# Cross-attention block with FFN: the residual of the quantised linears added to x by seven accumulating transfers instead of fourteen GpSimd additions

## The chip, the cores and the metric

The kernel runs on one core of one Trainium2 chip. The metric is device time in microseconds (us), taken as the median of several runs. The five engines of the core are TensorE (PE, with its weight loads shown apart as PEld), VectorE (DVE), ScalarE (ACT), GpSimd (POOL) and SyncE (SP). Each runs its own instruction stream in order, and they meet only through semaphores. Transfers run beside them on 16 DMA engines that all queues share.

## The reference, cut to what matters

```python
def smooth_quant_linear(x, w):            # x [T, D], w [O, D]
    s  = sqrt(max|x| over tokens / max|w| over rows)      # per column of D
    xs, ws = x / s, w * s
    x_q, w_q = round(xs / x_scale), round(ws / w_scale)   # scales per row, 127 levels
    return x_q @ w_q.T * x_scale * w_scale.T

def xattn(x, gate_up, ctx):               # 4 batches of 512 tokens, D = 512, I = 256
    gate, up = split(smooth_quant_linear(x, gate_up))
    return smooth_quant_linear(silu(gate) * up, ctx)

def ffn(x, ...):                          # all 2048 tokens
    pick 2 of 8 experts by the router logits summed over all tokens
    h = gelu(x @ w1[e] + b1[e]);  y = h @ w2[e] + b2[e]   # DFF = 2048
    return sum over the two experts of weight * y

x = x + xattn(layernorm(x), ...)          # the "+" is the residual of this change
x = x + ffn(layernorm(x), ...)
```

All data is float32.

## The kernel before, in words

Tokens lie on the 128 partitions, four tokens a partition and batch, so that `res` [128, 16, 512] holds x of all four batches. The program has two stages. The first, up to about 150 us, computes the two quantised linears of the four batches b = 0 to 3. The second, the FFN, works through 16 pairs of 128-wide hidden blocks; its products are split in high and low parts and multiplied with Strassen's seven products instead of eight.

The first stage is written out by hand: each engine has a list of steps such as `smooth_weight(2, 2)` (batch 2, linear 2) or `dequant(3, 2, 1)` (batch 3, linear 2, half 1), and runs them in that order. PSUM is used as four slots of two banks. Each slot has a fixed list of uses, and `drained` counts how many of them have been emptied; the helper `place` finds which slot and count a use such as `p2.1.0` (product of linear 2, batch 1, half 0) has.

The end of the first stage, for each batch: GpSimd rounds the second weight (`round_weight`, L372), TensorE transposes and multiplies (L616, L635), ScalarE copies the transposed integers out of PSUM (`integers_w`, L946), VectorE multiplies the product by its scales into `wv` (`dequant`, L1283). Then `add_residual(b, h)` (L385 to L391) on GpSimd adds half h (two of the four rows of 512 that a partition holds) of `wv` to `res`. Seven of the eight halves are done so; the last, (3, 1), is VectorE's `add_last_residual` (L1330).

The second layer norm follows. Its sums come from ScalarE for batch 0 (`moments(0, 2)`, L911 and L916) and from VectorE for batches 1 to 3 (L1217 to L1223). GpSimd's `inv_std` (L340, L341) turns them into the reciprocal of the standard deviation. The rows are normalised by ScalarE (L895), by GpSimd for batch 2 (L396) and by VectorE for half of batch 3 (L1323). TensorE transposes them (`normed2`, L656), the router's product (L667) and the choice of two experts follow, and with it SyncE's first loads of expert weights (L285, L289).

The order of GpSimd around the change is: `add_residual(0,0)`, then `smooth_weight(2,2)`, four small steps, `round_weight(1,2)`, `row_scale(2,2,1)`, `add_residual(0,1)`, `round_weight(2,2)`, `smooth_weight(3,2)`, `row_scale(3,2,0)`, `add_residual(1,0)`, `inv_std(0,2)`, `row_scale(3,2,1)`, `add_residual(1,1)`, `round_weight(3,2)`, `add_residual(2,0)`, `inv_std(1,2)`, `add_residual(2,1)`, `add_residual(3,0)`, `inv_std(2,2)`, `normalise(2)`, `inv_std(3,2)`. Those that read `res` next wait for `res_added[b]`, which each addition raises by one.

Of the kernel before, what the change touches and what calls it, by code (L numbers as in the profile page):

```python
# [5 lines left out]
ALU = mybir.AluOpType  # L6
# [17 lines left out]
def xattn_ffn(  # L24
# [16 lines left out]
    TT = T // P  # L41
# [3 lines left out]
    H = KD // 2  # L45
# [16 lines left out]
    with ExitStack() as ctx:  # L62
        def sb(name, shape, dt=F32, stack=ctx):
            return stack.enter_context(nc.sbuf_tensor(name, shape, dt))

        def sem(name):
            return ctx.enter_context(nc.semaphore(name))

        def each(name):
            return [sem(f"{name}{b}") for b in range(B)]  # L70
# [21 lines left out]
        def place(use):  # L92
            for i, uses in enumerate(SLOTS):
                if use in uses:
                    return i, uses.index(use)


        res = sb("res", [P, NT, D])
# [41 lines left out]
        def batch_sb(name, shape, dt=F32):  # L140
            return [sb(f"{name}{b}", shape, dt, early) for b in range(B)]
# [6 lines left out]
        wv = batch_sb("wv", [P, OT, D])  # L148
# [74 lines left out]
        xscale_ready, wscale_ready = each("xscale_ready"), each("wscale_ready")  # L223
        xr_ready, wr_ready = each("xr_ready"), each("wr_ready")
        silu_ready, a_ready, res_added = each("silu_ready"), each("a_ready"), each("res_added")
        hi_ready, lo_ready = each("hi_ready"), each("lo_ready")
        res_last, xn_last = sem("res_last"), sem("xn_last")
        part_ready, tok_ready, t4_sum = each("part_ready"), sem("tok_ready"), sem("t4_sum")
# [89 lines left out]
        def _(pool):  # L318
            g = nc.gpsimd
# [66 lines left out]
            def add_residual(b, h):  # L386
                slot_i, n = place(f"p2.{b}.{h}")
                pool.wait_ge(drained[slot_i], n + 1)
                for j in range(H * h, H * h + H):
                    r = res[:, b * TT + j, :]  # L390
                    g.tensor_tensor(r, r, wv[b][:, j, :], ALU.add).then_inc(res_added[b], 1)  # L391

            def normalise(b):
                pool.wait_ge(nmr_ready[b], 2)
# [50 lines left out]
            gate_up_product(3, 1)  # L445
            root(2, 2)
            add_residual(0, 0)
            smooth_weight(2, 2)
            row_scale(2, 2, 0)
# [3 lines left out]
            round_weight(1, 2)  # L453
            row_scale(2, 2, 1)
            add_residual(0, 1)
            round_weight(2, 2)
            smooth_weight(3, 2)
            row_scale(3, 2, 0)
            add_residual(1, 0)
            inv_std(0, 2)  # L460
            row_scale(3, 2, 1)
# [427 lines left out]
        def _(act):  # L889
# [10 lines left out]
            def summed(ins):  # L900
                sums[0] += 1
                ins.then_inc(mom_link, 1)
                act.wait_ge(mom_link, sums[0])

            def moments(b, c):
                if c == 1:
                    act.wait_ge(x_load[b], 16)
                for j in range(TT):
                    if c == 2:
                        act.wait_ge(res_added[b], j + 1)  # L910
                    ins = s.activation(xv[b][:, j, :], res[:, b * TT + j, :], ACT.Identity,  # L911
                                       accum_out=mv[b][:, j, 0:1])
                summed(ins)
                summed(s.mul(nmean[c - 1][b][:, :], mv[b][:, :, 0], -1.0 / D))
                for j in range(TT):
                    ins = s.activation(xv[b][:, j, :], res[:, b * TT + j, :], ACT.Square,  # L916
                                       bias=nmean[c - 1][b][:, j:j + 1], accum_out=mv[b][:, j, 1:2])
                summed(ins)
                s.activation(var_e[c - 1][b][:, :], mv[b][:, :, 1], ACT.Copy, bias=LN_EPS, scale=1.0 / D
                             ).then_inc(var_ready[b], 1)  # L920
# [89 lines left out]
            normalise(0, 1)  # L1010
            normalise(1, 1)
            moments(2, 1)
            keep_smooth_row(0, 1)
            moments(3, 1)
            normalise(2, 1)
            keep_smooth_row(1, 1)
# [48 lines left out]
            integers_w(1, 2, 0)  # L1065
            keep_scale_row(2, 2)
            moments(0, 2)
            integers_w(2, 2, 0)
            round_x(3, 2)
# [113 lines left out]
        def _(dve):  # L1183
# [4 lines left out]
            def link(ins):  # L1188
                chain[0] += 1
                ins.then_inc(dve_link, 1)  # L1190
                dve.wait_ge(dve_link, chain[0])
# [17 lines left out]
            def moments(b, c):  # L1209
                if c == 1:  # L1210
                    dve.wait_ge(x_load[b], 16)
                for j in range(TT):
                    if c == 2 and b == B - 1 and j >= H:
                        dve.wait_ge(res_last, j - H + 1)
                    elif c == 2:
                        dve.wait_ge(res_added[b], j + 1)
                    ins = v.bn_stats(stats[b][:, j, :], res[:, b * TT + j, :])  # L1217
                link(ins)
                for j in range(TT):
                    ins = v.bn_aggr(mv[b][:, j, :], stats[b][:, j, :])  # L1220
                link(ins)
                v.tensor_scalar(nmean[c - 1][b][:, :], mv[b][:, :, 0], -1.0, None, ALU.mult)
                v.tensor_scalar(var_e[c - 1][b][:, :], mv[b][:, :, 1], LN_EPS, None, ALU.add).then_inc(var_ready[b], 1)  # L1223
# [168 lines left out]
            dve.sem_inc(comb_ready, 15)  # L1392
            dve.sem_inc(h_ready, 4)
            moments(0, 1)
            amax_w(0, 0)
            moments(1, 1)
            amax_w(0, 1)
            amax_x(0, 0)
# [89 lines left out]
            dequant(2, 2, 0)  # L1488
            dequant(2, 2, 1)
            moments(1, 2)  # L1490
            dequant(3, 2, 0)
            dequant(3, 2, 1)
# [133 lines left out]
```

## Time and profile before

| what | value |
|---|---|
| median of three runs | 820.07 us (819.11 to 821.62) |
| profiled execution, its span | 818.7 us |
| what the median has above that span | 1.4 us |
| TensorE busy | 771.5 us, 94% |
| VectorE busy | 477.7 us, 58% |
| GpSimd busy | 449.7 us, 55% |
| ScalarE busy | 354.6 us, 43% |
| mean granted TensorE clock | 0.979 of full speed |

The span runs from the first to the last instruction of one profiled execution. For that execution no time is listed beside its span, so the span is its own time here. Busy shares are averages over both stages: in the page's 40 slices of 20.5 us, TensorE is at 50 to 80% in the first seven and at 90% or more from there on. A step of the first stage costs time only if it is on the chain that leads to the FFN's start.

### The profile page before, as it was taken

What the parts mean: (1) busy time and instruction counts of PE and PEld (TensorE: products, weight loads), DVE (VectorE), ACT (ScalarE), POOL (GpSimd) and SP (SyncE); (2) the same over time, 40 slices, a digit from 0 to 9 for tenths busy, and PEclk for the clock granted to TensorE, in tenths of its full rate; (3) what the DMA queues carried; (4) which work ended last, traced back from release to release, by engine and by line L of the source; (5) the groups of instructions that cost most, each with busy time, mean ns of one, the idle gap of its engine ahead of it and who ended that gap; (6) DMA issues with size and microseconds to landing.
All of it is one profiled execution on the core that took longest, in us unless ns stands there. A gap on an engine that the chain in (4) does not pass through costs nothing.

```text
span 818.7 us, 11342 instructions
## 1 busy us (share of the span) xinstructions
PE 771.5 (94%) x3570; PEld 624.1 (76%) x3577; DVE 477.7 (58%) x669; ACT 354.6 (43%) x660; POOL 449.7 (55%) x497
## 2 busy tenths in 40 slices
PE   5688666999999999999999999999999999999998
PEld 4666455688788888888888888888888888888886
DVE  5999759797754545454545454545454545454545
ACT  3967588743442434343424343434343434242422
POOL 1789997157564646464646464646464646464622
PEclk9899968999999999999999999999999999999999
DMA  9400000301010101010101010101010101010022
GB/s 344 173 2 1 1 0 2 129 1 51 1 52 1 51 0 49 3 50 2 48 4 51 1 45 6 42 9 44 7 41 11 36 15 36 15 32 19 0 103 104
DMA packets 19077, 32.34 MB, mean 39 GB/s; under 512 B 872, under 2 KB 11240, under 8 KB 18160
## 3 DMA queue, kind: packets, MB, share of 16 engines
q1 hardware_dynamic: 18896, 31.98, 11.1%
q8 instruction: 12, 0.20, 0.1%
q10 hardware_dynamic: 160, 0.08, 0.0%
q14 instruction: 9, 0.07, 0.0%
HBM read 27.87 MB, written 4.19 MB: 39 GB/s over the span
## 4 chain that ended last, share of the span: by engine, by line
PE 83%; POOL 8%; DVE 3%; issue 2%; ACT 2%; DMA 1%; ACTq 0%; POOLq 0%; DVEq 0%
PE slot L805 42%; PE slot L792 34%; PE slot L850 3%; POOL wv L366 2%; POOL xf L383 1%; PE slot L667 1%; POOL wv L372 1%; POOL cv L366 1%; PE slot L585 1%; DVE rmax L1226 1%; DMA b_rows<-in_L_ffn_b 1%; POOL rstd L340 1%; POOL h_lo L476 1%; DVE stats L1217 1%; DVE peak_x L1226 1%
## 5 line engine op out<-in xcount | busy, mean ns | idle before, releaser
L792 PE MATMUL slot<-xo,a_hi 128*128 128x512 f32 x840 | 259.1, 390 | 0.0
L1541 DVE SCALAR_TENSOR_TENSOR res<-slot,rw,res 128x512 f32<-128x512 f32 x256 | 178.5, 750 | 130.3 <-PE slot L805 130.2
L1570 DVE TENSOR_TENSOR e<-slot,e 128x512 f32<-128x512 f32 x150 | 103.8, 692 | 173.4 <-PE slot L792 173.3
L805 PE MATMUL slot<-w_hi,h_hi 128*128 128x512 f32 x512 | 201.3, 393 | 0.4 <-POOL h_lo L476 0.4
L805 PE MATMUL slot<-w_lo,h_hi 128*128 128x512 f32 x512 | 199.6, 390 | 0.0
L805 PE MATMUL slot<-w_hi,h_lo 128*128 128x512 f32 x512 | 199.4, 390 | 0.0
L792 PEld LDWEIGHTS slot<-xo,a_hi 128*128 128x128 f32 x840 | 157.4, 188 | 33.3 <-DVE e L1570 0.2
L476 POOL TENSOR_TENSOR h_lo<-e,h_hi 128x512 fp32r<-128x512 f32 x96 | 138.1, 1451 | 55.0 <-ACT e L1104 54.0
L792 PE MATMUL slot<-xo,a_lo 128*128 128x512 f32 x420 | 163.7, 390 | 0.0
L805 PEld LDWEIGHTS slot<-w_hi,h_hi 128*128 128x128 f32 x512 | 96.1, 188 | 25.1 <-POOL h_lo L476 5.6
L476 POOL TENSOR_TENSOR h_lo<-hid,h_hi 128x512 fp32r<-128x512 f32 x32 | 44.1, 1378 | 124.7 <-ACT hid L1104 124.7
L805 PEld LDWEIGHTS slot<-w_hi,h_lo 128*128 128x128 f32 x512 | 96.2, 188 | 20.1
L805 PEld LDWEIGHTS slot<-w_lo,h_hi 128*128 128x128 f32 x512 | 96.2, 188 | 19.3
L792 PEld LDWEIGHTS slot<-xo,a_lo 128*128 128x128 f32 x420 | 78.9, 188 | 16.5
L1103 ACT ACTIVATE h_hi<-e,b_now 128x512 fp32r<-128x512 f32 x90 | 64.9, 721 | 58.0 <-DVE e L1570 57.6
L1142 ACT COPY e<-slot 128x512 f32<-128x512 f32 x30 | 17.6, 587 | 164.5 <-PE slot L792 164.5
L490 POOL TENSOR_TENSOR a_lo<-raw,a_hi 128x256 fp32r<-128x256 f32 x45 | 34.3, 761 | 95.9 <-ACT a_hi L988 95.9
L991 ACT CAST w_hi<-raw 128x512 fp32r<-128x512 f32 x32 | 19.8, 622 | 109.8 <-PE slot L805 109.8
L495 POOL TENSOR_TENSOR w_lo<-raw,w_hi 128x512 fp32r<-128x512 f32 x30 | 38.7, 1289 | 50.4 <-ACT w_hi L991 50.4
L1104 ACT ACTIVATE e<-e,b_now 128x512 f32<-128x512 f32 x90 | 63.8, 709 | 0.0
L1103 ACT ACTIVATE h_hi<-slot,b_now 128x512 fp32r<-128x512 f32 x38 | 26.2, 689 | 66.5 <-PE slot L792 56.6
L490 POOL TENSOR_TENSOR a_lo<-ssum,a_hi 128x256 fp32r<-128x256 f32 x60 | 43.7, 739 | 0.0
(145 smaller groups left out, 814.5 us busy)
## 6 DMA issues: line engine op xcount, KB each, us to landing
raw<-in_L_ffn_w SPq DMA_DIRECT2D x32, 512.0 KB, 3.4
res<-in_x SPq DMA_DIRECT2D x4, 1024.0 KB, 11.9
wv<-in_fside_BxS2xS SPq DMA_DIRECT2D x4, 1024.0 KB, 12.8
out_x<-res SPq DMA_DIRECT2D x3, 1024.0 KB, 3.9
cv<-in_ctx SPq DMA_DIRECT2D x4, 512.0 KB, 13.1
out_x<-res SPq DMA_DIRECT2D x4, 256.0 KB, 2.7
b_row<-in_L_ffn_b SPq DMA_DIRECT2D x2, 256.0 KB, 4.6
b_rows<-in_L_ffn_b ACTq DMA_DIRECT2D x1, 64.0 KB, 6.0
```

Source lines behind the costliest of these rows:

```text
L366: g.tensor_tensor(w[:, j, :], w[:, j, :], rows[b][:, 0:n], ALU.mult).then_inc(wmul_ready[b], 1)
L476: g.tensor_tensor(h_lo[:, i, :], hid[i][:, :], h_hi[:, i, :].bitcast(F32), ALU.subtract).then_inc(h_ready, 1)
L490: g.tensor_tensor(a_lo[:, i, :, :], A_OF[i], a_hi[:, i, :, :].bitcast(F32), ALU.subtract).then_inc(a_ops_ready, 1)
L495: g.tensor_tensor(w2_lo[:, f, :], raw2[:, f, :], w2_hi[:, f, :].bitcast(F32), ALU.subtract).then_inc(w2_ready, 1)
L792: last = t.matmul(dst, a[:, i, k, :], xo[tp][:, v, k, :], start=(start and n == 0), stop=(n == 3 * H - 1), skip_group_check=True)
L805: last = t.matmul(y_bank[j][:, :], a[:, i, j * P:(j + 1) * P], v[:, f, :], start=(start and n == 0), stop=(not start and n == 2), skip_gro ...
L850: last = t.matmul(TILE_BANK[n], a[:, 2 * f + h, k, :], xo[q][:, v, k, :], start=(m == 0), stop=(m == 3 * KD - 1))
L991: s.copy(w2_hi[:, f, :], raw2[:, f, :]).then_inc(w2_hi_ready, 1)
L1103: s.activation(h_hi[:, i, :], src, ACT.Gelu_apprx_tanh, bias=bias).then_inc(hid_ready, 1)
L1104: s.activation(hid[i][:, :], src, ACT.Gelu_apprx_tanh, bias=bias).then_inc(hid_ready, 1)
L1541: v.scalar_tensor_tensor(out=r, in0=y_bank[j][:, :], scalar=rw[:, ds(p, 1), n:n + 1].rearrange("p a b -> p (a b)"), in1=r, op0=ALU.mult, o ...
L1570: v.tensor_tensor(dst[:, :], src, other[:, :], ALU.add).then_inc(comb_ready, 1)
```

## The change

A half's two additions by GpSimd, each of 128 x 512 elements, become one transfer, issued by GpSimd, that reads 128 x 1024 elements (512 KB) of `wv` and adds them to `res` at the destination. Its completion raises a semaphore by 16. There are now two semaphores for each batch, one for each half, and the readers wait for 16 on the one of their half. The order of steps on every engine stays as it was; VectorE's own addition of the last half stays too.

```diff
+        res_added2 = each("res_added2")
...
             def add_residual(b, h):
                 slot_i, n = place(f"p2.{b}.{h}")
                 pool.wait_ge(drained[slot_i], n + 1)
-                for j in range(H * h, H * h + H):
-                    r = res[:, b * TT + j, :]
-                    g.tensor_tensor(r, r, wv[b][:, j, :], ALU.add).then_inc(res_added[b], 1)
+                at = H * h
+                r = res[:, b * TT + at:b * TT + at + H, :]
+                g.dma_start(r, wv[b][:, at:at + H, :], accum_op=ALU.add).then_inc((res_added, res_added2)[h][b], 16)
...
                     if c == 2:
-                        act.wait_ge(res_added[b], j + 1)
+                        act.wait_ge((res_added, res_added2)[j // H][b], 16)
...
                     elif c == 2:
-                        dve.wait_ge(res_added[b], j + 1)
+                        dve.wait_ge((res_added, res_added2)[j // H][b], 16)
```

The instructions of GpSimd's queue from the rounding of batch 3's second weight to the second layer norm's last `inv_std`, before; the names ending in a digit are those of a batch:

```order
L391 TENSOR_TENSOR res<-res,wv 128x512 [waits drained2]
L391 TENSOR_TENSOR res<-res,wv 128x512
L372 TENSOR_SCALAR cv<-cv,rscale 128x256 [waits wscale_ready3]
L372 TENSOR_SCALAR cv<-cv,rscale 128x256 x3
L391 TENSOR_TENSOR res<-res,wv 128x512 [waits drained3]
L391 TENSOR_TENSOR res<-res,wv 128x512
L340 TENSOR_TENSOR rstd_1<-var_e_1,neg_half 128x4 [waits var_ready1]
L341 TENSOR_TENSOR nmr_1<-nmean_1,rstd_1 128x4 [waits pool_link]
L391 TENSOR_TENSOR res<-res,wv 128x512 [waits drained2]
L391 TENSOR_TENSOR res<-res,wv 128x512
L391 TENSOR_TENSOR res<-res,wv 128x512 [waits drained2]
L391 TENSOR_TENSOR res<-res,wv 128x512
```

The same place of GpSimd's queue now:

```order
L392 DMA res<-wv 128x1024 [waits drained2]
L373 TENSOR_SCALAR cv<-cv,rscale 128x256 [waits wscale_ready3]
L373 TENSOR_SCALAR cv<-cv,rscale 128x256 x3
L392 DMA res<-wv 128x1024 [waits drained3]
L341 TENSOR_TENSOR rstd_1<-var_e_1,neg_half 128x4 [waits var_ready1]
L342 TENSOR_TENSOR nmr_1<-nmean_1,rstd_1 128x4 [waits pool_link]
L392 DMA res<-wv 128x1024 [waits drained2] x2
```

Eight additions have become four DMA issues, those of (1,1), (2,0), (2,1) and (3,0). The issue for (2,1) still stands behind the `inv_std` of batch 1, which waits for that batch's variance.

## Rows read from the trace of the kernel before

**Rows 1.** The page's first and fourth parts: busy time, and the chain by engine.
```profile
PE 771.5 (94%) x3570; PEld 624.1 (76%) x3577; DVE 477.7 (58%) x669; ACT 354.6 (43%) x660; POOL 449.7 (55%) x497
...
PE 83%; POOL 8%; DVE 3%; issue 2%; ACT 2%; DMA 1%; ACTq 0%; POOLq 0%; DVEq 0%
```

**Rows 2.** Chain that ended last, in order: start us, us, what.
```profile
96.89 2.50 POOL res L391 x2
...
110.04 2.46 ACT xf L911 x8
...
133.58 3.05 POOL xf L396 x4
```

**Rows 3.** Groups by line and shape, 90 to 140 us: busy us, mean ns | idle before.
```profile
L391 POOL TENSOR_TENSOR res<-res,wv 128x512 f32<-128x512 f32 x14 | 17.5, 1271 | 0.3
```

**Rows 4.** Instructions in order of time, GpSimd: start us, us, what [idle before].
```profile
102.22 0.24 POOL L377 TENSOR_SCALAR scale<-rmax 128x4 f32<-128x4 f32 x1
...
106.80 2.49 POOL L391 TENSOR_TENSOR res<-res,wv 128x512 f32<-128x512 f32 x2
...
116.72 1.04 POOL L340 TENSOR_TENSOR rstd<-var_e,neg_half 128x4 f32<-128x4 f32 x1
...
118.43 2.50 POOL L391 TENSOR_TENSOR res<-res,wv 128x512 f32<-128x512 f32 x2
...
125.40 1.03 POOL L340 TENSOR_TENSOR rstd<-var_e,neg_half 128x4 f32<-128x4 f32 x1 [0.18 <-DVE var_e L1223]
...
126.66 4.97 POOL L391 TENSOR_TENSOR res<-res,wv 128x512 f32<-128x512 f32 x4
```

**Rows 5.** The same view, ScalarE.
```profile
111.16 0.62 ACT L911 ACTIVATE xf<-res 128x512 f32<-128x512 f32 x1
...
115.72 0.20 ACT L919 ACTIVATE var_e<-mv 128x4 f32<-128x4 f32 x1
```

**Rows 6.** The same view, VectorE.
```profile
100.63 1.22 DVE L1226 TENSOR_REDUCE rmax<-xf 128x4 f32<-128x1024 f32 x1
...
121.98 2.46 DVE L1217 BATCH_NORM_STATS2 stats<-res 128x6 f32<-128x512 f32 x4
...
125.74 2.73 DVE L1283 SCALAR_TENSOR_TENSOR wv<-slot,scale,wsc_row 128x512 f32<-128x512 f32 x4 [0.42 <-PE slot L635]
128.38 2.46 DVE L1217 BATCH_NORM_STATS2 stats<-res 128x6 f32<-128x512 f32 x4
...
132.84 2.46 DVE L1217 BATCH_NORM_STATS2 stats<-res 128x6 f32<-128x512 f32 x4
```

**Rows 7.** The same view, TensorE.
```profile
86.41 1.89 PE L635 MATMUL slot<-xf 128*128 128x512 bf16 x8
...
104.24 1.92 PE L606 MATMUL slot<-ident,xf 128*128 128x128 f32 x8
...
116.98 3.57 PE L635 MATMUL slot<-xf 128*128 128x512 bf16 x8 [4.56 <-ACT xf L946]
...
122.37 1.04 PE L616 MATMUL slot<-ident,cv 128*128 128x128 f32 x8
```

**Rows 8.** DMA view: issues by line, KB each, median us to landing.
```profile
GB/s 344 173 2 1 1 0 2 129 1 51 1 52 1 51 0 49 3 50 2 48 4 51 1 45 6 42 9 44 7 41 11 36 15 36 15 32 19 0 103 104
...
raw<-in_L_ffn_w SPq DMA_DIRECT2D x32, 512.0 KB, 3.4
...
out_x<-res SPq DMA_DIRECT2D x3, 1024.0 KB, 3.9
cv<-in_ctx SPq DMA_DIRECT2D x4, 512.0 KB, 13.1
out_x<-res SPq DMA_DIRECT2D x4, 256.0 KB, 2.7
```

**Rows 9.** Instructions in order of time, SyncE's queue.
```profile
148.99 0.39 SPq L285 DMA_DIRECT2D raw<-in_L_ffn_w  x1
```

**Rows 10.** Window 116.9 to 120.5 us: length, busy of PE, PEld, DVE, ACT, POOL, PEclk, DMA, GB/s.
```profile
116.90:120.50 3.60, 3.52 (x9) 1.40 (x10) 1.59 (x3) 3.60 (x8) 3.35 (x5) 0.50 0.00 0
```

## The prediction

> **What bounds the kernel now.** I read the page's busy times first: TensorE is busy 94% of the span and carries 83% of the chain of waits, with GpSimd second at 8% [rows 1]. The FFN is TensorE's and the change leaves it alone, so all that can move is its start, and the FFN then shifts as a block. The chain in order of time says what sets that start: between 97 and 137 us it goes from GpSimd over ScalarE back to GpSimd [rows 2]. One addition pair, that of (0,0) at 96.89 us, is a link of the chain itself. The reader should see that ScalarE's sums of batch 0 at 110.04, which read what the additions write, are a link too, and so is GpSimd's normalising at 133.58. Then I read each engine's instructions in order of time, to find how long before its reader each addition is done.
>
> **What is removed.** Fourteen additions of 1.271 us, 17.5 us of GpSimd in all [rows 3], 2.5 us a half. Seven issues take their place. How long an issue holds GpSimd no row shows. From below it is SyncE's issue, 0.39 us [rows 9]; above that lies the pair that it replaces, 2.5 us, or even the whole transfer (a rival below). I take 1.1 us more than the landing of a SyncE transfer would include, from one addition of 1.27 us as the nearest GpSimd work over 128 partitions.
>
> **Where removing it pays.** The pair at 96.89 delays `smooth_weight(2,2)` and so the row scale at 102.22. That needs VectorE's maximum, which starts at 100.63 and takes 1.22 us [rows 4, 6]; with 0.08 us of handing over it could start at 101.93. So 2.5 us less of work is worth at most 102.22 - 101.93 = 0.3 us. The pair at 106.80 lies before `round_weight(2,2)`, but the product that this feeds waits for ScalarE until 116.98 [rows 7], because the copy out of PSUM stands behind ScalarE's whole `moments(0,2)`, which ends at 115.72 + 0.20 = 115.92 [rows 5]. Nothing there. Later GpSimd gets 2 us ahead in `round_weight(3,2)`, but its transposes start at 122.37 without a wait, behind TensorE's own work [rows 7]. Nothing again. From 125.40 GpSimd waits for VectorE's variance of batch 1 [rows 4]. The gain is 0.3 us in all.
>
> **What a transfer costs.** Call L the time from the start of GpSimd's issue until the reader sees the semaphore. No row shows an accumulating transfer. The nearest is the plain load of 512 KB by SyncE, 3.4 us [rows 8]. An addition at the destination must read the destination too, 512 KB more. By the stores (1024 KB in 3.9 us, 256 KB in 2.7) that is 2 x 0.4 = 0.8 us; by the rate of the loads in the first slice, 344 GB/s, it is 1.5 us [rows 8]. I take 1.5, and 1.1 for the issue as above: L = 3.4 + 1.5 + 1.1 = 6.0 us. From below L is no less than the 2.7 us of a 256 KB store; from above 13.1 us is the context load of the same size, in a crowded queue [rows 8].
>
> The Trainium skill, "DMA: Bandwidth & Descriptors", Anatomy of one DMA (SWDGE, gpsimd path), fits a GpSimd-issued transfer as 2.0 us plus bytes over 436 GB/s. For 512 KB that estimate is 3.2 us, close to the row's 3.4 us for SyncE's; if the destination's read counts in full it is 4.4 us. No run here shows either yet. By these L would sit at the low end, and the sum below would be about 0 to +1 us.
>
> **Where the landing is awaited.** Four readers matter. Before, the addition itself took 2.5 us; now it takes L.
>
> (a) Half (0,1), read by ScalarE's third sum at 111.16 [rows 5]. It is issued at 106.80 - 0.3 = 106.5. It stalls ScalarE if 106.5 + L > 111.16, that is L > 4.66. Then `integers_w(2,2)`, the product at 116.98 and all behind it shift. The shift is s = L - 4.66, and never below -0.3. At L = 6: +1.34.
>
> (b) Half (1,1), read by VectorE's third statistic of `moments(1,2)`, 1.19 us after 121.98, so at 123.17 (+ s) [rows 6]. Its issue follows `inv_std(0,2)`, which waits for the variance at 115.92 [rows 5] where it was at 116.72 before. From there to the old pair it was 118.43 - 116.72 = 1.71 us [rows 4], so it is issued at 117.65 + s. The stall is L - 5.5. At L = 6: +0.5.
>
> (c) Half (2,1), read by VectorE's third statistic of `moments(2,2)`, at 128.38 + 1.19 = 129.57 [rows 6]. Its issue cannot move forward, because `inv_std(1,2)` is ahead of it in the queue and waits for VectorE until 125.40; so it stays at 126.66 [rows 4]. Before, the pair was done at 126.66 + 2.49 = 129.15, 0.4 us ahead of the reader. Now it lands at 126.66 + L. The stall is L - 2.9. At L = 6: +3.1. Nothing covers it. Behind the waiting statistic stand VectorE's last residual, `moments(3,2)`, the low parts, and behind those GpSimd's `inv_std`s and `normalise(2)` at 133.58, TensorE's transposes and the router: the whole way to the FFN.
>
> (d) Half (3,0), issued right behind (2,1), is read 132.84 - 129.57 = 3.3 us after it [rows 6]. One issue and the second transfer's own movement (1.5 x 2 us) fit in that. Nothing.
>
> The other halves cost nothing up to L = 7.7. (0,0) has 13 us, from 96.89 to 109.9. The pair (1,0) stood ahead of the `inv_std` at 116.72, so it began by 114.2, 7.8 us before its reader at 121.98. The pair (2,0) stood ahead of 125.40, so it began by 122.9, and now begins 2.2 us earlier (the issue at 117.65 in place of 118.43, and 1.1 us in place of 2.5): 7.7 us before 128.38 [rows 2, 4, 6].
>
> **The sum.** At L = 6: 1.34 + 0.5 + 3.1 = +4.9 us, of which the second term is partly absorbed by the 0.42 us that VectorE waited before the product at 125.74, but it comes back through `inv_std(1,2)`, so I keep it. Against the profiled execution, 818.7 + 4.9 = 823.6 us. The median of the runs stood 1.4 us above that span: 825.0 us. The slope is steep, one to three us for each us of L: L = 3.4 gives -0.3 + 0.5 = +0.2; L = 5 gives +2.4; L = 7 gives 2.3 + 1.5 + 4.1 = +7.9; L = 9 gives 4.3 + 3.5 + 6.1 = +13.9.
>
> TensorE's clock adds an uncertainty of its own. After 4.56 us of idle the product at 116.98 ran 3.57 us at clock 0.50, the lower level; eight matmuls of that kind took 1.89 us at 86.41, half as much [rows 7, 10]. A longer idle makes this no better, and may slow the transposes behind it. I leave it out of the sum and put +-1.7 us beside it.
>
> **Rivals.**
> 1. The transfer lands nearly as a plain one does, L between 3 and 5: the stalls (a) and (b) are small, (c) is 0.1 to 2.1. The rows for it are the 3.4 and 3.9 us of plain transfers [rows 8], and hardly anything else moves on the DMA engines then. Against it stands the second read and that GpSimd has to produce the issue. Time: 820.0 to 822.5 us, no change that can be told. The Trainium skill's fit above lies here.
> 2. The transfer is much slower, L of 8 or more, or GpSimd is held for the whole of it. If held at L = 6, `smooth_weight(2,2)` comes 3.5 us late, (0,1) lands at 106.8 + 3.5 + 6 = 116.3, 5.1 us after its reader; (c) costs 3.1, and (3,0) starts only when (2,1) is done, 6 - 3.3 = 2.7 more: 5.1 + 3.1 + 2.7 = +10.9, and 831 us. In this case GpSimd isn't relieved and the change doesn't do what it says. Unheld with L = 8 it is also +10.9. For it: nothing in the rows excludes it; an in-place addition is not shown at all. Against it: 512 KB is little for 16 engines.
> 3. Faster: L below about 4, and TensorE's gap of 4.56 us before 116.98 gets shorter by the 0.3 us and stays at the upper clock. Then the product costs 1.7 us less, and the transposes at 104.24, 1.92 us against 1.04 us for eight of the same size at 122.37, cost 0.9 less [rows 7]: -0.3 - 1.7 - 0.9 = -2.9, 817.2 us. It decides where L is below 4.66 (no stall of ScalarE) and the gap falls short of whatever lowers the clock; 0.3 us off 4.56 is a weak reason.
>
> **How the numbers follow.** Chances: my forecast (L of 5 to 8) 0.46, rival 1 0.32, rival 2 0.18, rival 3 0.04. The likeliest case gives 825.0 us, its own range 822.4 to 831. A measurement of this kernel can tell 0.3%, 2.5 us, from no change. Faster by more is rival 3, 0.04; within it is rival 1 with the low edge of mine, 0.32; slower is the rest, 0.64. The range takes in rival 1 from its middle and rival 2 up to 834: 820.3 to 834.
>
> **What would show it.** In the changed profile: the issue at L392 as a group of seven with its time to landing (my 6.0 less the hand-over); ScalarE's L912 waiting for a DMA at about 111 us by 1 to 2 us; VectorE's L1218 waiting for a DMA of `res` at about 130 us, some 3 us; GpSimd's busy time down by about 17 us at no gain; the FFN from TensorE's L851 on of the same length, and started 5 us later. Wrong would be: a landing under 4.5 us with no such waits, GpSimd idle or blocked for the length of a transfer at L392, or a first FFN matmul that starts earlier than before.

## The result and the profile after

The change made the kernel slower, by a third of a per cent: 823.0 us median of 17 runs against 820.07 of the kernel before, ratio 1.0032, 95% interval 1.0021 to 1.0043, that is 2.6 us; the two medians differ by 2.9. One of the 17 runs of the kernel before took 1304.35 us, and nothing here rests on it. The runs of the changed kernel also list their spans. The median span is 821.1 us, and the time lies 1.9 us above the span. The same holds for 35 runs of the kernel before that were taken beside the first experiments: 1.9 us above a median span of 818.1. The span shown in front of the prediction, 818.7, lies above its median, and that of the profile after, 819.8, below its own: this pair of profiles tells less than half of the loss in its spans, so what follows reads waits, and takes totals from the runs.

The page after, parts 1 and 6. GpSimd is busy 9.8 us less, not 17.5, because the seven issues count as its work (6.6 us) and its `normalise(2)` takes 1.0 us more, as shown below; the transfers land after 4.7 us.

```profile
PE 770.1 (94%) x3570; PEld 622.7 (76%) x3577; DVE 477.2 (58%) x669; ACT 354.4 (43%) x660; POOL 439.9 (54%) x490
...
raw<-in_L_ffn_w SPq DMA_DIRECT2D x32, 512.0 KB, 3.3
...
res<-wv POOLq DMA_DIRECT2D x7, 512.0 KB, 4.7
```

The instructions of GpSimd in the changed kernel, in order of time: start us, us, what [idle before]. They answer to [rows 4].

```profile
96.60 1.10 POOL L392 DMA_DIRECT2D res<-wv  x1
...
101.67 0.23 POOL L378 TENSOR_SCALAR scale<-rmax 128x4 f32<-128x4 f32 x1 [0.95 <-DVE rmax L1227]
...
106.22 0.95 POOL L392 DMA_DIRECT2D res<-wv  x1
...
115.74 1.04 POOL L341 TENSOR_TENSOR rstd<-var_e,neg_half 128x4 f32<-128x4 f32 x1 [2.69 <-ACT var_e L920]
...
117.44 0.97 POOL L392 DMA_DIRECT2D res<-wv  x1
...
124.95 1.04 POOL L341 TENSOR_TENSOR rstd<-var_e,neg_half 128x4 f32<-128x4 f32 x1 [3.62 <-DVE var_e L1224]
...
126.35 1.81 POOL L392 DMA_DIRECT2D res<-wv  x2
133.17 1.40 POOL L341 TENSOR_TENSOR rstd<-var_e,neg_half 128x4 f32<-128x4 f32 x1 [5.02 <-DVE var_e L1224]
...
134.96 4.07 POOL L397 TENSOR_SCALAR xf<-res,rstd,nmr 128x512 f32<-128x512 f32 x4
139.00 1.97 POOL L341 TENSOR_TENSOR rstd<-var_e,neg_half 128x4 f32<-128x4 f32 x1
```

GpSimd now waits where it worked: 0.95, 2.69, 3.62 and 5.02 us idle, each time for a value of VectorE or ScalarE. Beyond the 0.3 us of the row scale at 101.67 its freed time buys nothing. And its four rows of `normalise(2)` (L397), 3.05 us in [rows 2], take 4.07.

The same view of VectorE and ScalarE in the changed kernel, to lay beside [rows 5, 6]. This execution is 0.28 us ahead of that of before already at 93 us, where nothing has changed yet; that is to be added to its times.

```profile
127.99 1.28 DVE L1218 BATCH_NORM_STATS2 stats<-res 128x6 f32<-128x512 f32 x2
131.11 1.29 DVE L1218 BATCH_NORM_STATS2 stats<-res 128x6 f32<-128x512 f32 x2 [1.83 <-DMA res<-wv]
...
134.20 2.46 DVE L1218 BATCH_NORM_STATS2 stats<-res 128x6 f32<-128x512 f32 x4
...
137.26 2.85 DVE L1292 TENSOR_TENSOR xo<-xf,xo 128x1024 fp32r<-128x1024 f32 x2
```

```profile
110.53 0.20 ACT L912 ACTIVATION_READ_ACCUMULATOR xf<-res 128x1 f32 x1
110.88 0.63 ACT L912 ACTIVATE xf<-res 128x512 f32<-128x512 f32 x1
...
115.44 0.20 ACT L920 ACTIVATE var_e<-mv 128x4 f32<-128x4 f32 x1
```

VectorE's third statistic of batch 2 waits 1.83 us for the transfer of half (2,1): issued at 126.35, seen at 131.11, so 4.76 us. ScalarE's third sum starts 0.15 us after the read before it has ended, where it overlapped that by 0.1 us in [rows 5]: 0.25 us lost on half (0,1), issued at 106.22 and seen at 110.88 (4.66 us).

The FFN itself did not change: from its first matmul (L850 before, L851 now) to the end of the span it is 665.2 us in both, and in the profiles of the first four experiments too. The first stage makes the whole difference.

The chain of waits of the changed kernel, in order of time, names the same two transfers:

```profile
106.22 4.63 DMA res<-wv
110.88 1.35 ACT xf L912 x4
...
126.35 4.74 DMA res<-wv
131.11 1.30 DVE stats L1218 x2
...
134.96 4.07 POOL xf L397 x4
```

### The profile page after: what moved, and what is told of

Read it like the earlier page. It is cut to its first block, busy times and chain, and to the rows that moved or that the text cites. A ratio compares the mean times of both kernels' runs of the same rounds, so it can differ in the third digit from the quotient of the medians.

```text
span 819.8 us, 11335 instructions
## 1 busy us (share of the span) xinstructions
PE 770.1 (94%) x3570; PEld 622.7 (76%) x3577; DVE 477.2 (58%) x669; ACT 354.4 (43%) x660; POOL 439.9 (54%) x490
## 4 chain that ended last, share of the span: by engine, by line
PE 81%; POOL 9%; DVE 4%; issue 3%; DMA 2%; ACT 1%; ACTq 0%; POOLq 0%; DVEq 0%
PE slot L806 42%; PE slot L793 34%; PE slot L851 3%; POOL wv L367 2%; DMA res<-wv 1%; POOL xf L384 1%; POOL wv L373 1%; POOL cv L367 1%; PE slot L586 1%; DVE rmax L1227 1%; POOL rstd L341 1%; DVE stats L1218 1%; DMA b_rows<-in_L_ffn_b 1%; POOL h_lo L477 1%; DVE peak_x L1227 1%
```

## The experiments

Theory A at the start: the loss is landing time that readers wait for, nearly all of it half (2,1), whose issue stands behind an `inv_std` that waits. Theory B: a price for using the transfers at all, outside the readers' waits. Ratios are to the kernel before, run on the same chip, with 95% intervals.

**Transfer of (2,1) ahead of the inv_std of batch 1.**

```diff
             add_residual(2, 0)
-            inv_std(1, 2)
             add_residual(2, 1)
+            inv_std(1, 2)
```

> The changed kernel with one GpSimd step moved: the transfer of half (2,1) is issued ahead of the inv_std of batch 1 instead of behind it. Theory A (the loss is the landing time of (2,1), 4.76 us counted from an issue that waits behind inv_std): the issue comes at about 121.9 us instead of 126.35, lands near 126.6, VectorE's wait of 1.83 us at 131.1 is gone, GpSimd's normalise(2) no longer meets VectorE's low parts for its whole length (3.05 us again, not 4.07), and the time falls from the changed kernel's by 2 to 2.7 us, to the kernel before or 0.3 us under it (ratio 0.999 to 1.001). Theory B (the loss is a fixed price of having a seventh kind of queue, the software one, or of the transfers disturbing other engines): the wait goes but the time stays 1 us or more above the kernel before (ratio 1.0015 or more).

Measured: 0.9991 (0.9976 to 1.0005). The issue comes at 122.64. The wait for (2,1) is gone; one of 0.46 us for (3,0) is left, because that transfer took 5.7 us. One order of two steps is worth 0.4%, the whole loss: for A. How that 0.4% divides is another question. In its profile `normalise(2)` is back at 3.03 us, and TensorE's granted clock between 140 and 143 us is 1.00 where it is 0.50 in the kernel before and in the changed one. Below, VectorE and GpSimd of this run:

```profile
128.79 2.46 DVE L1218 BATCH_NORM_STATS2 stats<-res 128x6 f32<-128x512 f32 x4
...
133.60 2.47 DVE L1218 BATCH_NORM_STATS2 stats<-res 128x6 f32<-128x512 f32 x4 [0.46 <-DMA res<-wv]
...
136.85 2.35 DVE L1292 TENSOR_TENSOR xo<-xf,xo 128x1024 fp32r<-128x1024 f32 x2
```

```profile
133.82 3.03 POOL L397 TENSOR_SCALAR xf<-res,rstd,nmr 128x512 f32<-128x512 f32 x4
137.02 1.91 POOL L341 TENSOR_TENSOR rstd<-var_e,neg_half 128x4 f32<-128x4 f32 x1 [0.17 <-DVE var_e L1224]
```

**Only (2,1) added by GpSimd.** `if (b, h) not in MOVED:` the two additions as before, with MOVED all of the seven but (2,1).

> The changed kernel with only half (2,1) added by GpSimd as before, the other six by transfer. Theory A: the additions run from 126.3 to 128.8, VectorE doesn't wait, half (3,0) is issued at 128.8 and lands at 133.5, while it is read at 132.6: a wait of about 0.9 us takes the place of the 1.9, so the ratio to the kernel before is 1.0005 to 1.0015 and VectorE shows one wait for the transfer of (3,0). Theory B: ratio as of the changed kernel, 1.002 to 1.004.

Measured: 0.9990 (0.9976 to 1.0004), lower than A's range. In its profile VectorE waits 2.47 us for (3,0), more than the 0.9 expected, and yet the loss is gone. Two things can explain it, and the runs don't tell which. The wait comes one step later: GpSimd's `normalise(2)`, started by the variance of batch 2, went ahead meanwhile (133.27, 3.03 us, no collision). And the profiled execution, with a span of 819.8, was the slowest of the twelve, whose median is 817.5; its transfer took 6.1 us, which may not be so in most.

**An idle queue.** The kernel before, with one 2 KB transfer issued by GpSimd at 13 us, and a wait for it behind GpSimd's last step of the first stage (the declarations are left out here):

```diff
             inv_std(0, 1)
+            link(g.memset(spare2[:, :], 0.0))
+            g.dma_start(spare[:, :], spare2[:, :]).then_inc(spare_in, 16)
...
             inv_std(3, 2)
+            pool.wait_ge(spare_in, 16)
```

> The kernel before, all fourteen additions by GpSimd, plus one plain transfer of 2 KB that GpSimd issues at about 13 us into its idle time and that nobody reads. Theory A: no change in the span (ratio 1.0000 within 0.0005). Theory B: the use of a queue for GpSimd's transfers has a price outside the span or at its end; the time less the span grows by 0.5 us or more and the ratio is 1.0005 to 1.002.

Measured: 0.9998 (0.9985 to 1.0012), time less span 1.91 us, as without it. B is out as far as such a queue has a fixed price.

**Only (2,1) by transfer.** The reverse: MOVED is (2,1) alone, and the other six halves are added by GpSimd.

> The kernel before with only half (2,1) turned into a transfer, six halves still added by GpSimd. Theory A: this one transfer carries the whole loss. It is issued at 126.66 and lands at 131.4, against 129.57 for its reader, +1.9 us of wait; the additions of (3,0) run 127.6 to 130.1 and are in time. Ratio 1.002 to 1.004, the same as the changed kernel or 0.0003 above it (it lacks the 0.3 us gained by the other halves). Theory B: about a seventh of the loss, ratio under 1.001.

Measured: 1.0041 (1.0029 to 1.0053). One transfer of seven carries the whole loss. That the other six give anything back is not shown: this interval overlaps that of the changed kernel. Its profile has the same picture as the changed kernel: issue at 127.09, reader at 131.89, `normalise(2)` 4.08 us. So A is shown from both sides: without (2,1) no loss, with (2,1) alone all of it.

**What the landing consists of.** Three kernels, each timed once. First the addition left out (`accum_op=ALU.add` removed, so that `wv` is copied over `res`); then these copies issued by SyncE, with GpSimd doing neither additions nor issues; then the accumulating transfers cut into two of 256 KB each.

> The changed kernel with plain copies of wv over res in place of the accumulating transfers: same shapes, same GpSimd issues, but the residual's addition is left out. Theory A (the addition at the destination halves the rate at which 16 engines move the data, and that is the larger part of the landing time): DMA windows of a single transfer show about twice 197 GB/s, and the landing falls from 4.7 to 3.2 to 3.5 us. Theory B (the landing is mostly GpSimd's issue and the completion): 4.2 us or more.

> The same plain copies issued by SyncE, each behind a wait for its product's last drain; the residual's addition is left out, and GpSimd has neither additions nor issues. Theory A: SyncE's issue takes 0.4 us instead of 0.9 and the landing is 0.8 to 1.1 us shorter than in the run with GpSimd's copies, 2.3 to 2.7 us; that difference is the part of the landing that belongs to GpSimd making the transfer. Theory B: no difference, under 0.3 us.

> The changed kernel with each transfer cut in two, 256 KB each, fourteen in all, both of a half raising one semaphore to 32. Theory A (landing is a fixed part of about 2.0 us plus 512 KB at 197 GB/s, 2.7 us): a first piece lands after 3.3 us, a second one, behind it, after about 4 us; GpSimd's issue takes 0.9 us again for each piece, so the whole half lands 0.3 us later than the 4.7 us of one transfer. Theory B (landing independent of size): each piece 4.5 us or more.

Measured: 3.0 us to landing for GpSimd's copies, 2.9 for SyncE's, 4.7 for the accumulating ones; pieces of 256 KB land after 3.3 us at the least and 4.2 at the median, and the half (2,1) as a whole after 5.35 us (issued at 127.58, seen at 132.93). The DMA columns of the windows view (last three: clock, share of 16 engines, GB/s) show where the difference is. First the changed kernel, its first transfer, issued at 96.60; then the run with copies, issued at 96.71:

```profile
97.60:98.60 1.00, 0.72 (x7) 0.48 (x5) 1.00 (x2) 0.44 (x2) 0.75 (x2) 1.00 0.39 74
98.60:99.60 1.00, 0.00 (x0) 0.00 (x0) 1.00 (x2) 0.84 (x1) 1.00 (x3) 1.00 1.12 217
99.60:100.60 1.00, 0.00 (x0) 0.00 (x0) 0.97 (x2) 0.00 (x0) 1.00 (x2) 1.00 1.05 197
100.60:101.60 1.00, 0.00 (x0) 0.00 (x0) 0.98 (x1) 0.00 (x0) 0.12 (x1) 0.60 0.21 37
```

```profile
98.00:98.50 0.50, 0.43 (x4) 0.19 (x2) 0.50 (x2) 0.00 (x0) 0.44 (x1) 1.00 0.90 360
98.50:99.00 0.50, 0.00 (x0) 0.00 (x0) 0.50 (x1) 0.47 (x1) 0.50 (x2) 1.00 1.02 410
99.00:99.50 0.50, 0.00 (x0) 0.00 (x0) 0.50 (x2) 0.50 (x1) 0.50 (x2) 1.00 0.70 279
```

After the start of the issue nothing moves for 1.3 us in the copy and 1.6 us in the addition. Then all 16 engines are busy: at 410 GB/s for a copy, at 197 GB/s with the addition. 512 KB take 1.3 us at the one rate and 2.7 at the other, which is 1.4 of the 1.7 us between the landings; the later start is the other 0.3. The theory on the rate is shown; that on GpSimd's issue isn't: 3.0 against 2.9 us is 0.1, not 0.8 to 1.1. An issue holds GpSimd 0.95 us (0.6 for a copy, and SyncE 0.46), but little of that shows in the landing. The pieces took 1.13 us of issue each, and ahead of the last of them GpSimd stood for 2.9 us, which the chain of that run puts down to "issue":

```profile
130.32 2.92 issue
133.23 3.28 DMA res<-wv
136.53 2.48 DVE stats L1219 x4
```

In this run cutting the transfers up was no way out: VectorE waited 2.00 us for (2,1). The single times were 820.9 us for the copies, 816.3 for SyncE's and 823.1 for the pieces; nothing rests on them.

**Halves chosen by slack.** Transfers for (0,0), (1,0), (1,1), (2,0) and (2,1), the last ahead of `inv_std(1,2)`; (0,1) and (3,0) added by GpSimd.

> The halves chosen by their slack: (0,0), (1,0), (1,1), (2,0) and (2,1) by transfer, (2,1) issued ahead of the inv_std of batch 1, and (0,1) and (3,0) added by GpSimd, which is idle there. No engine waits for a transfer. Theory A: the 0.15 us of ScalarE and the 0.46 us of VectorE that the run with (2,1) ahead still waited are gone as well; ratio to the kernel before 0.997 to 0.9995, and 0.3 to 0.8 us under the run with (2,1) ahead. Theory B (GpSimd's own later work, normalise(2) and inv_std(3,2), ends last anyway): 0.9985 to 1.0005, no better than the run with (2,1) ahead.

Measured: 0.9993 (0.9976 to 1.0010). VectorE and ScalarE wait for no transfer, and it is no better than the run with (2,1) ahead: theory B of that expectation. `normalise(2)` took 4.09 us in its profile, which leads to the next question.

**The two low parts later.** `keep_lo` is VectorE's subtraction that leaves the low part of a split tile (L1292 in the changed kernel). In all profiles so far the first of them starts 2.3 to 2.4 us after `normalise(2)` where VectorE doesn't wait for half (3,0). Where it was 2.29 to 2.32 us (the changed kernel, the idle queue, only (2,1), the copies, the mixed one) GpSimd took 4.07 to 4.09; where it was 2.40 or more (the kernel before, SyncE's copies, and the three runs in which `moments(3,2)` came later) it took 3.01 to 3.05. The fourth row starts 2.29 us after the first. In the changed kernel that row alone lasts 1.83 us, against 0.76 of the other three. The two sides are 0.1 us apart, and the idle queue, which has none of the transfers, is on the side of the changed kernel. First VectorE's row of the kernel before, 2.40 us after its `normalise(2)` at 133.58; then GpSimd and VectorE of the idle queue, 2.32 us apart:

```profile
135.98 2.86 DVE L1291 TENSOR_TENSOR xo<-xf,xo 128x1024 fp32r<-128x1024 f32 x2
```

```profile
134.50 4.09 POOL L397 TENSOR_SCALAR xf<-res,rstd,nmr 128x512 f32<-128x512 f32 x4
...
136.82 2.85 DVE L1295 TENSOR_TENSOR xo<-xf,xo 128x1024 fp32r<-128x1024 f32 x2
```

So the seven transfers are not needed for the two to collide. Three more runs move VectorE's work away from GpSimd's: the changed kernel, the changed kernel with (2,1) ahead, and the kernel before, each with this edit.

```diff
-            keep_lo(0, 0)
-            keep_lo(1, 0)
             normalise_last()
+            keep_lo(1, 0)
             token_sums(2)
             keep_lo(1, 1)
             token_sums(3)
             token_total()
+            keep_lo(0, 0)
             keep_lo(0, 1)
```

> The changed kernel with VectorE's two first low parts, keep_lo(0,0) and keep_lo(1,0), moved behind its normalise_last. Question: does the 1.0 us by which GpSimd's fourth row of normalise(2) is longer (1.83 instead of 0.76 us) come from VectorE's subtraction beside it, and does it count? Theory A (it does): GpSimd's normalise(2) takes 3.0 us in place of 4.07, the reciprocal root of batch 3 behind it 1.0 us in place of 1.97, VectorE's wait of 1.8 us for the transfer stays, and the time falls by 1 to 2 us: ratio to the kernel before 1.0005 to 1.0025. Theory B (the lengthening is of GpSimd's own making, or what GpSimd gains is lost because the low parts come later to the router): normalise stays at 4 us, or ratio 1.0025 or more.

> Both moves: (2,1)'s transfer ahead of the inv_std of batch 1, and the two low parts behind normalise_last. Theory A: neither VectorE's wait nor the collision is left; ratio to the kernel before 0.997 to 0.9985. Theory B: 0.9985 to 1.0005, as of the run with only the transfer ahead.

> The kernel before, all additions by GpSimd, with only the two low parts moved. It tells what of the run with both moves belongs to the transfers. Theory A: its normalise(2) takes 3.0 us and the root 1.0 to 1.4, ratio 0.998 to 0.9995; the run with both moves lies 0 to 0.8 us under it, since the transfers' own worth is the 0.3 us of the prediction and a little room on GpSimd. Theory B: ratio 0.9995 to 1.001.

Measured: the changed kernel with it 1.0009 (0.9997 to 1.0022), both moves 0.9989 (0.9977 to 1.0001), the kernel before with it 0.9994 (0.9982 to 1.0005). GpSimd of the first of these, and VectorE:

```profile
134.47 3.03 POOL L397 TENSOR_SCALAR xf<-res,rstd,nmr 128x512 f32<-128x512 f32 x4
137.47 1.01 POOL L341 TENSOR_TENSOR rstd<-var_e,neg_half 128x4 f32<-128x4 f32 x1
```

```profile
130.61 1.29 DVE L1218 BATCH_NORM_STATS2 stats<-res 128x6 f32<-128x512 f32 x2 [1.97 <-DMA res<-wv]
...
138.79 1.00 DVE L1324 TENSOR_SCALAR xf<-res,rstd,nmr 128x512 f32<-128x512 f32 x2 [1.94 <-POOL nmr L342]
```

The wait for the transfer is still there, 1.97 us, while `normalise(2)` is back at 3.03 us and the root behind it (the first step of `inv_std(3,2)`) at 1.01 instead of 1.97. So the collision is real, and it is caused by VectorE's subtraction beside GpSimd's work. The ratio of the changed kernel falls from 1.0032 to 1.0009, 1.9 us, and the intervals just touch. That those 1.9 us are all the collision's is not shown. The same edit takes the root from 1.97 to 1.00 us in the kernel before, whose profile had no collision in `normalise(2)`, and it lets TensorE's clock rise earlier: between 140 and 143 us 0.95 of full speed is granted in the changed kernel with it, 0.50 without.

These three runs were taken side by side, so their medians can be compared. With the low parts out of the way, (2,1) late costs 820.69 - 819.15 = 1.5 us against (2,1) ahead; with the low parts early the same two orders are 0.41%, 3.4 us, apart. So about 1.5 us go with the wait by itself, and the rest with what it meets behind it, the collision and TensorE's clock. Each of the ratios behind these numbers carries about 1 us either way, so the split is an estimate. Against a large share of the collision by itself stands the run with the halves chosen by slack: its profile has the collision and no wait, and its ratio is 0.9993.

With both moves the point estimate is the lowest of the study, 0.9 us under the kernel before. It falls under theory B of its expectation, no better than with only the transfer ahead. Its interval touches 1, and that of the kernel before with the low parts moved overlaps it: no version was shown to beat the kernel before.

## Why the prediction was right in its direction and too high in its size

Forecast 825.0 us, measured 823.0; +4.9 forecast, +2.6 to +2.9 measured. The place and the mechanism were right, the main size was wrong: L, and the effect of a shift on the engines behind it. Step by step:

- *Where removing it pays*: right. The 0.3 us at 101.93 is there (the row scale at 101.67 after 0.95 us of idle, its time 0.28 us early as the whole execution is), and nothing else; the two later places gave nothing, and GpSimd waits there now.
- *What a transfer costs*: the step that was mis-sized. L was set at 6.0 and is 4.7. Of its three terms the second read was about right: 1.5 forecast, 1.7 between the landings of copy and addition, 1.4 of it movement. The base was too high: 3.4 us was a load from memory outside the core, and a copy inside SBUF issued by SyncE lands in 2.9. And the 1.1 us for GpSimd's issue were 0.1 between the two kinds of copy.
- *The estimate beside it*: the Trainium skill, "DMA: Bandwidth & Descriptors", Anatomy of one DMA (SWDGE path), gives an estimate of 3.2 us for such a transfer: the copies' 3.0 agrees. With the destination's read counted in full the estimate is 4.4, close to the measured 4.7, and closer than my sum of rows. I wrote that the sum would then be 0 to +1 us; by my own formulas an L of 4.4 gives +1.2.
- *(a), half (0,1)*: formula right, input wrong. At L = 4.66 it gives s = 0, and the trace has it so: a wait of 0.25 us ate the gain of 0.3.
- *(b), half (1,1)*: the same. L is below 5.5, and VectorE doesn't wait.
- *(c), half (2,1)*: right in place and reason. L - 2.9 is 1.9 at L = 4.76, the trace shows 1.83, and the two opposite experiments give the whole loss to this half.
- *(d), half (3,0)*: right that it costs nothing in the changed kernel. Issued at 127.1 it lands after 6.4 us, because it moves behind (2,1): the windows of the changed kernel (below; last column GB/s) are full from 128 to 133 us without a pause. Two times 512 KB at 197 GB/s take 5.3 us, and the margin left to its reader at 134.20 is 0.7 us. In another order it is waited for.

```profile
130.00:131.00 1.00, 0.61 (x6) 0.37 (x4) 0.00 (x0) 1.00 (x5) 0.00 (x0) 1.00 1.02 197
...
132.00:133.00 1.00, 0.00 (x0) 0.00 (x0) 0.93 (x8) 1.00 (x5) 0.00 (x0) 1.00 1.03 201
133.00:134.00 1.00, 0.00 (x0) 0.00 (x0) 1.00 (x4) 1.00 (x2) 0.83 (x1) 1.00 0.02 0
```

- *What was missing*: the price of the shift itself. VectorE and GpSimd behind the wait don't move as a block. With the 0.28 us added, `normalise(2)` starts 1.66 us late in the changed profile, and ScalarE's normalising of batch 3, which waits for the root behind it (138.93 before, 141.28 now), 2.63 us late: the 1.0 us between them is the longer fourth row. How much of the loss is due to it in the mean of runs stays open, since the idle queue shows the collision without any of the seven transfers.
- *TensorE's clock*: left out of the sum, with +-1.7 us beside it, and the profiles differ by about as much. From the start of batch 3's transposes to the FFN's first matmul it is 13.7 us in the kernel before, 12.4 in the changed one, 11.5 with (2,1) ahead and 14.2 with only (2,1) by transfer. The 16 transposes took 3.87 us in the kernel before, at a granted clock of 0.50, and with (2,1) ahead fourteen of them took 1.75, at 1.00. So the changed profile got 1.3 us back there, and its FFN starts only 1.05 us later than before (1.3 with the 0.28), where 5 was forecast.
- *The 1.4 us above the span*: 1.9 in the runs that list it. My 818.7 came from an execution 0.6 us above the median span.

The first rival, a landing between 3 and 5, was the right one in L (4.7), and by my sum would have given 818.7 + 1.9 + 1.4 = 822.0 us, 1.0 under the measured time; the collision that it lacked is of that size. My likeliest case asked for an L of 5 to 8, which did not come. That 823.0 still lies in that case's own range of 822.4 to 831, and above the 822.5 of this rival, is luck: terms that the sum did not have made up for a part of an L that was too high. The sign of a GpSimd busy time down by 17 us did not come either (9.8), and ScalarE's wait was 0.25 us instead of 1 to 2.

## What to carry to other kernels

Ask of every piece of work that goes to a DMA how long its reader can wait from the issue on, not what it frees: six of these halves had the 4.7 us, one of them only just, the seventh had 2.9, and it took the gain of all. Then ask what the issue is queued behind; here moving it ahead of one waiting step undid the loss. And look for neighbours before taking a delay as rigid: here two engines missed each other by 0.1 us in one profile and met in others, and a step of 3.0 us took 4.1 where they met.

## What the hardware showed that I had not expected

The addition at the destination about halves the rate: 197 GB/s against 410, with all 16 engines busy either way.

A transfer can have a tail. In the run with (2,1) added by GpSimd, the transfer of (3,0), alone in its queue, was issued at 128.94 and seen at 135.06, 6.1 us. Its windows and its DMA view:

```profile
132.40:132.90 0.50, 0.00 (x0) 0.00 (x0) 0.18 (x1) 0.50 (x3) 0.47 (x1) 1.00 0.99 188
132.90:133.40 0.50, 0.00 (x0) 0.00 (x0) 0.00 (x0) 0.50 (x2) 0.33 (x2) 1.00 0.09 8
133.40:133.90 0.50, 0.00 (x0) 0.00 (x0) 0.00 (x0) 0.50 (x2) 0.50 (x1) 1.00 0.08 16
133.90:134.40 0.50, 0.22 (x2) 0.20 (x2) 0.00 (x0) 0.50 (x1) 0.50 (x2) 1.00 0.08 16
134.40:135.00 0.60, 0.34 (x3) 0.15 (x2) 0.00 (x0) 0.60 (x2) 0.60 (x2) 1.00 0.00 0
```

```profile
q0 software_dynamic: 144, 0.52, 34.6%
q8 instruction: 1, 0.02, 1.2%
```

After 132.9 about one engine of sixteen is busy, for 1.5 us more. In the same 8 us one packet of the instruction queue took 1.2% of 16 engines, 1.5 us; narrower windows place it between 130.4 and 131.0, while the transfer moves. The changed kernel had no packet of that queue between 126.3 and 135 us, and its two transfers there had no such tail. The transfer of 5.7 us with (2,1) ahead had such a packet beside it, between 128.2 and 128.6, and so had the copy of (2,0) by SyncE, between 121.3 and 121.8; that copy landed after 5.0 us instead of 2.9. That this fetch of code held up one engine's share of the transfer fits these numbers; no run removed the packet to test it.
